# Four of eight batches: a hardware loop against the same passes written out

## The chip, the core and the metric

The kernel runs on one core of a Trainium2 chip. The metric is device time in microseconds (us); the kernel before takes 741.31 us, the median of three runs (741.03 to 741.88).

A core has five engines with an instruction stream each, synchronised by semaphores: TensorE (PE, with its weight loads shown as PEld), VectorE (DVE), ScalarE (ACT), GpSimd (POOL) and SyncE (SP), which here only issues transfers.

## The reference, cut to what matters

The input x is 8 batches of 1024 nodes with 128 features; adj is one 1024 x 1024 matrix that all batches share. Four layers follow one another in each batch, each added to its input and normalised over the 128 features:

```python
x = layernorm(x + L0(x, adj))   # (adj@x + x)@w0 + b0, rows scaled to length 1
x = layernorm(x + L1(x, adj))   # exp(8*tanh(q.k/sqrt(128)/8)) * adj, rows scaled to sum 1, @x @v
x = layernorm(x + L2(x, adj))   # (si + sj + adj*w_r + g_b) @ x @ w2 + b2
x = layernorm(x + L3(x, adj))   # relu(sum_k T_k(Laplacian of adj) @ x @ w3[k] + b3)
```

No batch depends on another, and every batch has the same work.

## The kernel before

The nodes are eight chunks of 128. Float32 products are made of float16 parts: `split_product` (lines 1113 to 1117) issues three matmuls for one product (high by high, high by low, low by high). TensorE therefore gets 7478 matmuls and as many weight loads.

Each engine has its own program, a function under `@block.sync`, `@block.gpsimd`, `@block.scalar`, `@block.vector` or `@block.tensor`. In each, a function `body(i, nxt, cur, prev, last)` issues one pass. Pass i is a software pipeline over three batches and a half: layer 0 of batch i+1 (flag `nxt`), the attention of batch i (`cur`), layers 2 and 3 of batch i-1 (`prev`), and the last residual and store of batch i-2 (`last`). The order of the instructions in a pass is written out by hand; engines meet only through semaphores, and nothing joins all of them between passes.

`iterations(eng, body)` (line 201) puts the passes in sequence: -1 fills the pipeline, 0, 1 and 2 are written out, 3 to 6 are one body in a hardware loop on each engine (line 208), and 7 is written out, followed by a written tail that drains the pipeline. Passes 2 and 3 to 6 have all four flags set, and their instructions are the same but for the values. Pass 1 still carries some Laplacian preparation.

Semaphores only count up over the whole run, so the value waited for grows with i:

```python
pe.wait_ge(S["pl"], t8 + t + 1)        # t8 = i * C, C = 8
```

On TensorE a pass begins with `scores(0)` (line 1207), the products of x1T and gr, shown as `r<-gr,x1T`. It ends with `apply_laplacian(r0, xq, ...)` (line 1382), shown as `r<-xq,lap`. So on TensorE the loop's branch lies between a matmul `r<-xq,lap` and a matmul `r<-gr,x1T`. On DVE a pass begins with `end_sum` (line 739) and `x0_max`, on ACT with the first tanh (line 391).

Of the kernel before, what the change touches and what calls it, by code (L numbers as in the profile page):

```python
# [12 lines left out]
B, N, D = 8, 1024, 128  # L29
# [62 lines left out]
def adj_resnorm(nc, x, adj, w0, b0, q, k, v, gw, gb, w2, b2, w3, b3, out):  # L92
    ctx = ExitStack()
    with ctx:
# [106 lines left out]
        def iterations(eng, body):  # L201

            body(-1, True, False, False, False)
            body(0, True, True, False, False)
            body(1, True, True, True, False)
            body(2, True, True, True, True)
            with eng.Fori(3, B - 1) as i:
                body(i, True, True, True, True)
            body(B - 1, False, True, True, True)  # L210

# [3 lines left out]
        @block.sync  # L215
        def _(sp):
            sp.dma_start(x0[:], x_v[0]).then_inc(S["x_in"], 16)
            adj_v = adj.rearrange("(c p) m -> c p m", p=P)
            for c in range(C):
                sp.dma_start(adj_rows[:, c, :], adj_v[c]).then_inc(adj_in[c], 16)  # L220
                if c == 1:
                    for dst, src in ((b0_bc[:], b0), (b2_bc[:], b2), (b3_bc[:], b3.rearrange("a b d -> (a b d)")),
                                     (wj_bc[:], gw[0:D]), (wi_bc[:], gw[D:2 * D]),
                                     (wr_gb[:, 0:1], gw[2 * D:2 * D + 1]), (wr_gb[:, 1:2], gb)):
                        sp.dma_start(dst, src.partition_broadcast(P)).then_inc(S["w_in"], 16)
            out_v = out.rearrange("b (c p) d -> b p c d", p=P)

            def body(i, nxt, cur, prev, last):
                if nxt and cur:
                    sp.wait_ge(S["e0"], i + 1)  # L230
                    sp.dma_start(x0[:], x_v[i + 1]).then_inc(S["x_in"], 16)
                if last:
                    sp.wait_ge(S["ln3_a"], i - 1)
                    sp.dma_start(out_v[i - 2], outb[:]).then_inc(S["stored"], 16)

            iterations(sp, body)
            sp.wait_ge(S["ln3_a"], B - 1)
            sp.dma_start(out_v[B - 2], outb[:]).then_inc(S["stored"], 16)
            for h, (first, end) in enumerate(END_PARTS):
                sp.wait_ge(S["ln3_v"], h + 1)  # L240
                sp.wait_ge(S["ln3_a"], B + h)
                sp.dma_start(out_v[B - 1][:, first:end], z_end.outb[:, first:end]).then_inc(S["stored"], 16)
            sp.wait_ge(S["stored"], 16 * (B + 1))
# [3 lines left out]
        def _(pool):  # L247
# [15 lines left out]
            def body(i, nxt, cur, prev, last):  # L263
# [14 lines left out]
                if cur:  # L278
                    norm_root(1, i)

            iterations(pool, body)
            norm_root(2, B - 2)
            norm_root(3, B - 3)
# [11 lines left out]
        def _(act):  # L295
# [68 lines left out]
            def body(i, nxt, cur, prev, last):  # L364
# [107 lines left out]
                if cur:  # L472
                    copy_x2(i)

            iterations(act, body)

            y2_hi(B - 2, 1)
# [992 lines left out]
```

## Time and profile before

| | |
|---|---|
| time, median of 3 runs | 741.31 us (741.03 to 741.88) |
| span of the profiled execution | 740.6 us |
| own time of the profiled execution | not given apart from its span; the median is 0.71 us above the span |
| PE busy | 648.8 us, 88% |
| DVE busy | 616.4 us, 83% |
| ACT busy | 384.0 us, 52% |
| POOL busy | 70.4 us, 10% |
| mean granted clock of TensorE | 0.959 of full |

The span runs from the first to the last instruction. A busy share is an average over all stages. Register, branch and semaphore instructions are not counted as busy; the view of one source line lists them under the engine's name with a q (PEldq is TensorE's sequencer). "issue" as the releaser of an idle time means that the profile shows no instruction of another engine that was waited for.

### The profile page before, as it was taken

How to read it: one execution, taken by the hardware profiler on the slowest of the kernel's cores; microseconds unless marked ns; L12 is line 12 of the kernel's file. 1: busy time of each engine (PE TensorE's matmuls, PEld its weight loads, DVE VectorE, ACT ScalarE, POOL GpSimd, SP SyncE). 2: the span in 40 equal slices, each digit the busy share in tenths (PEclk: the TensorE clock that was granted, in tenths of full speed). 3: DMA queues.
4: the chain of work that ended last, by engine and by line, in shares of the span. 5: the costliest groups of instructions: out<-in, count | busy, mean ns of one | idle time of the engine just before them, and what ended most of it. 6: DMA issues, size and time to landing. Idle time of an engine off the chain costs nothing.

```text
span 740.6 us, 17928 instructions
## 1 busy us (share of the span) xinstructions
PE 648.8 (88%) x7478; PEld 490.0 (66%) x7478; DVE 616.4 (83%) x1562; ACT 384.0 (52%) x525; POOL 70.4 (10%) x49
## 2 busy tenths in 40 slices
PE   3936955899999999999899998999899999949895
PEld 3533633566876687668757785668766786636894
DVE  3789898998989899989879896989788897887526
ACT  3828906763468255924395444915393447541302
POOL 0020001001200120011100210012000210020001
PEclk8989987999999999999999999999999999979998
DMA  8000000000100020002000020002000000001001
GB/s 264 38 29 1 1 1 29 1 1 2 31 2 1 1 59 2 2 1 59 4 1 2 1 59 2 2 1 58 4 1 2 22 10 1 2 1 30 2 3 58
DMA packets 20013, 14.59 MB, mean 20 GB/s; under 512 B 864, under 2 KB 18912, under 8 KB 19936
## 3 DMA queue, kind: packets, MB, share of 16 engines
q1 hardware_dynamic: 18816, 12.91, 5.9%
q8 instruction: 64, 1.05, 0.6%
q10 hardware_dynamic: 1120, 0.52, 0.2%
q14 instruction: 13, 0.11, 0.1%
HBM read 9.24 MB, written 4.19 MB: 18 GB/s over the span
## 4 chain that ended last, share of the span: by engine, by line
issue 42%; DVE 23%; PE 22%; ACT 5%; POOL 5%; DMA 1%; SPq 1%; POOLq 0%; ACTq 0%; DVEq 0%
POOL small L256 5%; PE r L1115 5%; PE r L1117 5%; PE r L1116 5%; DVE p_lo L791 3%; DVE att L786 3%; DVE stats L522 3%; ACT att L391 2%; DVE x L944 1%; DMA lap<-in_adj 1%; DVE x L561 1%; DVE lap L673 1%; PE m L1115 1%; PE m L1117 1%; PE m L1116 1%
## 5 line engine op out<-in xcount | busy, mean ns | idle before, releaser
L256 POOL TENSOR_TENSOR small<-small,minus_half 128x8 f32<-128x8 f32 x39 | 66.0, 1698 | 618.6 <-DVE small L544 494.8
L391 ACT ACTIVATE att<-r,coef 128x1024 f32<-128x1024 f32 x64 | 70.5, 1101 | 60.7 <-PE r L1117 60.4
L1229 PE MATMUL av<-vhi,p_hi 128*128 128x129 f16 x512 | 89.7, 220 | 6.9 <-DVE p_lo L791 6.5
L1232 PE MATMUL av<-vhs,p_lo 128*128 128x129 f16 x512 | 89.5, 220 | 0.0
L1231 PE MATMUL av<-vlo,p_hi 128*128 128x128 f16 x512 | 89.5, 219 | 0.0
L786 DVE TENSOR_TENSOR att<-att,adjT 128x1024 f32<-128x1024 f32 x64 | 78.1, 1220 | 10.8 <-ACT att L393 10.8
L791 DVE SCALAR_TENSOR_TENSOR p_lo<-p_hi,att 128x1024 f16<-128x1024 f16 x64 | 77.9, 1219 | 0.0
L1115 PE MATMUL r<-gr,lap 128*128 128x128 f16 x448 | 75.9, 219 | 0.0
L1117 PE MATMUL r<-gr,lap 128*128 128x128 f16 x448 | 75.8, 219 | 0.0
L1116 PE MATMUL r<-gr,lap 128*128 128x128 f16 x448 | 75.8, 219 | 0.0
L1115 PE MATMUL r<-xq,lap 128*128 128x128 f16 x448 | 75.4, 219 | 0.0
L1116 PE MATMUL r<-xq,lap 128*128 128x128 f16 x448 | 75.4, 219 | 0.0
L1117 PE MATMUL r<-xq,lap 128*128 128x128 f16 x448 | 75.4, 219 | 0.0
L303 ACT ACTIVATE p_hi<-att 128x1024 f16<-128x1024 f32 x64 | 66.8, 1044 | 6.5 <-DVE att L786 6.2
L393 ACT ACTIVATE att<-att 128x1024 f32<-128x1024 f32 x64 | 67.7, 1058 | 2.0
L1229 PEld LDWEIGHTS av<-vhi,p_hi 128*128 128x128 f16 x512 | 50.0, 98 | 19.9 <-DVE p_lo L791 15.7
L1115 PE MATMUL r<-gr,x1T 128*128 128x512 f16 x128 | 49.9, 390 | 11.5 <-issue 7.5
L331 ACT ACTIVATE x<-x,small 128x128 f32<-128x128 f32 x69 | 28.9, 481 | 50.6 <-DVE small L554 50.6
L1231 PEld LDWEIGHTS av<-vlo,p_hi 128*128 128x128 f16 x512 | 50.1, 98 | 4.2
L522 DVE BATCH_NORM_STATS2 stats<-x 128x6 f32<-128x128 f32 x248 | 51.7, 279 | 0.9
L1115 PE MATMUL m<-a_hi,x2s 128*128 128x512 f16 x128 | 49.3, 385 | 1.5 <-DVE r2b L700 0.8
L1232 PEld LDWEIGHTS av<-vhs,p_lo 128*128 128x128 f16 x512 | 50.1, 98 | 0.0
(294 smaller groups left out, 1932.0 us busy)
## 6 DMA issues: line engine op xcount, KB each, us to landing
x<-in_x SPq DMA_DIRECT2D x8, 512.0 KB, 4.4
lap<-in_adj SPq DMA_DIRECT2D x8, 512.0 KB, 9.6
out<-outb SPq DMA_DIRECT2D x7, 512.0 KB, 4.5
out<-att SPq DMA_DIRECT2D x1, 384.0 KB, 2.8
b_bc<-in_L_gnn_bias SPq DMA_DIRECT2D x3, 64.0 KB, 7.4
x<-in_L_gnn_weight ACTq DMA_DIRECT2D x1, 192.0 KB, 8.3
out<-att SPq DMA_DIRECT2D x1, 128.0 KB, 2.7
x<-in_L_gnn_q ACTq DMA_DIRECT2D x1, 64.0 KB, 4.1
```

Of the source, the lines that this page charges most:

```text
L256: return nc.gpsimd.tensor_tensor(dst, src, minus_half[:], ALU.pow)
L391: nc.scalar.activation(att[:, s], (r1, r0)[t % 2][:], ACT.Tanh, scale=c_tanh).then_inc(S["th"], 1)
L393: nc.scalar.activation(att[:, s], att[:, s], ACT.Exp, scale=TANH_CAP).then_inc(S["ex"], 1)
L522: l_ = nc.vector.bn_stats(stats[:, k_, j].rearrange("p a k -> p (a k)"), src[:, j])
L786: tt(att[:, s], att[:, s], adjT[:, t, :], ALU.mult).then_inc(S["pm"], 1)
L791: stt(p_lo[:, s], p_hi[:, s], -LO_UP, att[:, s], ALU.mult, ALU.add).then_inc(S["pl"], 1)
L1115: mm(dst, s_hi, m_hi, start=start, stop=False, skip_group_check=True)
L1116: mm(dst, s_hi, m_lo, start=False, stop=False, skip_group_check=True)
L1117: return mm(dst, s_lo, m_hi, start=False, stop=stop, skip_group_check=True)
L1229: mm(acc, p_hi[:, s, chunk(j)], vhi[:, t, 0:D + 1], start=(t == 0 and j % 3 == 0), stop=False, skip_group_check=True)
L1231: mm(acc[:, 0:D], p_hi[:, s, chunk(j)], vlo[:, t, :], start=False, stop=False, skip_group_check=True)
L1232: l_ = mm(acc, p_lo[:, s, chunk(j)], vhs[:, t, 0:D + 1], start=False, stop=(t == C - 1), skip_group_check=True)
```

## The change

The loop statement becomes a Python loop, so the four passes are issued one after the other with constant i, as the others are. Blank lines at the top of the file go too; they make no instruction.

```diff
             body(2, True, True, True, True)
-            with eng.Fori(3, B - 1) as i:
+            for i in range(3, B - 1):
                 body(i, True, True, True, True)
             body(B - 1, False, True, True, True)
```

It holds for all five engines, since all call `iterations`. The data instructions and their order stay; the loop's register moves, additions, compares and branches go, and every computed wait value becomes a constant.

## Rows read from the trace of the kernel before

**Rows 1.** The page's first part: busy us (share of the span) and instructions of each engine

```profile
PE 648.8 (88%) x7478; PEld 490.0 (66%) x7478; DVE 616.4 (83%) x1562; ACT 384.0 (52%) x525; POOL 70.4 (10%) x49
```

**Rows 2.** Waits of PE, 137 to 613 us: waiter <- releaser: total us, times, longest

```profile
PE r L1115 <- issue: 7.5, 3, 2.6
PE r L1121 <- DVE x L561: 5.8, 6, 1.0
PE r L1115 <- DVE yT L677: 3.3, 6, 0.5
PE av L1229 <- DVE p_lo L791: 1.7, 2, 1.2
```

**Rows 3.** Windows from each pass's first scores matmul to the next's, passes 2 to 6

```profile
core 0: us, PE busy (x) PEld busy (x) DVE busy (x) ACT busy (x) POOL busy (x), PEclk, DMA share, GB/s
209.20:287.80 78.60, 77.04 (x927) 58.63 (x925) 71.02 (x183) 43.83 (x61) 8.55 (x5) 1.00 0.06 15
287.80:369.15 81.35, 77.24 (x929) 58.57 (x925) 72.97 (x185) 43.83 (x61) 8.52 (x5) 1.00 0.05 15
369.15:451.69 82.54, 78.57 (x925) 59.14 (x925) 71.20 (x183) 44.06 (x61) 8.52 (x5) 0.98 0.06 14
451.69:534.41 82.72, 78.57 (x924) 59.01 (x925) 71.20 (x183) 43.83 (x61) 8.52 (x5) 0.98 0.05 14
534.41:613.10 78.69, 77.07 (x924) 58.61 (x925) 69.24 (x181) 43.82 (x61) 8.52 (x5) 1.00 0.03 8
```

**Rows 4.** Line 208, the loop: engine op: duration ns min/median/max, first and last start

```profile
L208 SPq COMPARE_BRANCH  x4: 40/45/50, 344.1 to 590.7; - x4
L208 POOLq COMPARE_BRANCH  x4: 40/45/54, 351.9 to 598.5; - x4
L208 ACTq COMPARE_BRANCH  x4: 40/45/54, 358.1 to 604.7; - x4
L208 DVEq COMPARE_BRANCH  x4: 50/60/67, 364.7 to 611.3; - x4
...
L208 PEldq COMPARE_BRANCH  x4: 76/3348/3473, 365.6 to 612.2; - x4
```

**Rows 5.** Line 208 again, 600 to 620 us: TensorE's branch that is not taken

```profile
L208 PEldq COMPARE_BRANCH  x1: 76/76/76, 612.2 to 612.2; - x1
```

**Rows 6.** Timeline of PE around the pass ends: start us, us, what [idle before <-releaser]

```profile
366.46 0.22 PE L1117 MATMUL r<-xq,lap 128*128 128x128 f16 x1
369.15 0.39 PE L1115 MATMUL r<-gr,x1T 128*128 128x512 f16 x1 [2.46 <-issue]
...
451.69 0.61 PE L1115 MATMUL r<-gr,x1T 128*128 128x512 f16 x1 [2.46 <-issue]
...
534.41 0.39 PE L1115 MATMUL r<-gr,x1T 128*128 128x512 f16 x1 [2.59 <-issue]
...
613.05 0.22 PE L1117 MATMUL r<-xq,lap 128*128 128x128 f16 x1
613.10 0.38 PE L1115 MATMUL r<-gr,x1T 128*128 128x512 f16 x1
```

**Rows 7.** Windows right behind the three taken branches, columns as in the passes' windows

```profile
369.40:372.80 3.40, 3.40 (x10) 1.20 (x9) 0.00 (x0) 1.02 (x1) 0.00 (x0) 0.50 0.02 5
...
451.30:454.70 3.40, 3.01 (x8) 1.10 (x9) 0.00 (x0) 0.16 (x1) 0.00 (x0) 0.50 0.02 5
...
534.40:537.80 3.40, 3.39 (x32) 1.95 (x33) 0.07 (x1) 1.77 (x2) 0.00 (x0) 1.00 0.02 5
```

**Rows 8.** DMA queue of instructions, 209.2 to 287.8 us (pass 2): packets, MB, share

```profile
q8 instruction: 7, 0.11, 0.6%
```

**Rows 9.** The same queue, 369.15 to 451.69 us (pass 4, ends in a taken branch)

```profile
q8 instruction: 9, 0.15, 0.7%
```

**Rows 10.** Windows of pass 1 and of the tail, columns as in the passes' windows

```profile
137.30:209.20 71.90, 68.71 (x869) 54.14 (x868) 66.89 (x159) 35.63 (x48) 6.92 (x4) 1.00 0.03 9
...
652.70:663.00 10.30, 4.99 (x38) 4.62 (x39) 9.13 (x41) 4.13 (x9) 3.95 (x3) 0.50 0.00 0
...
693.70:697.10 3.40, 3.40 (x36) 3.40 (x34) 1.88 (x4) 1.19 (x2) 0.00 (x0) 0.50 0.00 0
```

## The prediction

> **What bounds the kernel now.** I read the page's first part, then the waits of TensorE, then a table of windows with one row for each pass, and only then the loop's own instructions, line by line and in the timeline.
>
> The first part shows PE busy for 648.8 us and DVE for 616.4 us of a span of 740.6 [rows 1]. Both are near full, so the question in the middle of the program is which one gives the pace. The waits answer it: between 137 and 613 us PE stands still in only four kinds of places, and the largest sum, 7.5 us in three waits, has no releaser on another engine [rows 2]. The other three kinds are waits for DVE of at most 1.2 us. PE is the pace, with short hand-overs to DVE in it.
>
> The windows give the length of a pass, measured on PE from the first scores matmul of one pass to that of the next [rows 3]. Pass 2 is written out and takes 78.60 us. Pass 3, the first in the loop, takes 81.35, pass 4 82.54, pass 5 82.72, and pass 6, which leaves the loop without branching back, 78.69. They hold the same data instructions (924 to 929 recorded matmuls each, a few records may be missing). So three of the loop's passes are 2.7 to 4.1 us longer than a written one, and they are the three that end in a taken branch.
>
> Where does the time lie? Line 208 answers: on SP, POOL, ACT and DVE the loop's branch takes 40 to 67 ns all four times; on TensorE it takes 3348 ns in the median and 3473 at most [rows 4], and 76 ns the one time that it is not taken [rows 5]. PE's queue still has matmuls in it when the branch begins at 365.6, and runs them until the last start at 366.46; the first of the next pass starts at 369.15, and the timeline puts 2.46 us of idle time before it, with no releaser. The same at 451.69 (2.46) and 534.41 (2.59). At the loop's exit the last matmul starts at 613.05 and the next at 613.10: no gap [rows 6].
>
> **What the branch costs, in two terms and a small one.**
>
> First the stall. From start to start the gap is 369.15 - 366.46 = 2.69 us instead of 613.10 - 613.05 = 0.05, so 2.64 us are lost on the engine that gives the pace; the third, by its idle time, costs 0.13 more. Sum: 2.64 + 2.64 + 2.77 = 8.05 us.
>
> Second the clock. Behind the first two stalls the granted clock is 0.50 for 3.40 us, the lower of its levels (1.2 GHz, against 2.4), behind the third it stays at 1.00 [rows 7]. What that does is read from whole passes, since waits absorb part of it: pass 4 holds such a stretch and a stall, pass 3 a stall of the same 2.46 us alone: 82.54 - 81.35 = 1.19 us. Pass 5 has a stretch too and a stall longer by 0.13: 82.72 - 81.35 - 0.13 = 1.24. Sum: 2.43 us.
>
> Third the register instructions that compute wait values in each loop pass. Pass 6 has them and neither stall nor slow clock: 78.69 - 78.60 = 0.09 us, times four passes = 0.36. I take 0.09 as it stands, although the two windows were cut to a hundredth; between 0 and 0.2 per pass it would move the sum by -0.4 to +0.4.
>
> The terms add to 8.05 + 2.43 + 0.36 = 10.84. The same sum without splitting: passes 3 to 6 last 613.10 - 287.80 = 325.30, four written passes 4 x 78.60 = 314.40, difference 10.90 us [rows 3]. I use 10.90.
>
> **What lies beside the path.** The branch, addition and register set-up of SP, POOL, ACT and DVE go as well; at some 50 ns each, with DVE busy 71.02 of the 78.60 us of a written pass and the others less [rows 3], their ends are covered by PE's work, and I cost them at nothing beyond the 0.09. If that cover were gone, four engines by four times 0.05 is under 1 us in all. No transfer is moved against the data instructions; the stores and loads of batches come at the same place of each pass, only 3 to 4 us sooner.
>
> What is late next when the stall goes? That needs no model: pass 2 is exactly the pass that the four become, with its own waits inside it (some 1.0 us for the DVE normalisation and 0.5 for yT, once each per pass, [rows 2]). DVE has 7.6 us of slack per pass, so it doesn't become the bound.
>
> What is added is program text: three more passes of instructions on every engine. An executed instruction has to be fetched in either form. Pass 2, straight, brought 7 packets of instructions [rows 8], and pass 4, which jumps back, 9 [rows 9]. So written out there are fewer packets, not more, and no pass's code was kept from the last time. In pass 2 those 7 packets left no idle time without a releaser: all three such waits are at the branches [rows 2].
>
> The Trainium skill, page "Runtime: NRT & Kernel Launch", section "Instruction fetch mechanics", says that a taken branch out of the fetched window forces a fetch before the engine can go on, while sequential prefetch is mostly hidden. The rows above show both halves here (3348 ns taken, 76 ns not taken, no idle time in a straight pass), and the sum by this rule is the one above. The Trainium skill's page "Advanced Engine Details and Errata", section "Control Flow Timing", gives some 108 ns for a compare-and-branch; by it three back edges would cost 0.3 us and the kernel would take about 741.0. TensorE's 3348 ns disagrees with it; the 40 to 67 ns of the others don't.
>
> **The tail** is the same code. Its granted clock is 0.50 in 652.70 to 663.00 and again in 693.70 to 697.10 [rows 10], behind idle times of PE. The program reaches the tail 10.9 us sooner, and where such a stretch begins and ends need not shift by just that. One stretch of 3.40 us more or less costs or gives at most 1.2 to 1.7 us (1.2 as above; 1.7, half of 3.40, if PE is never waited out). I take zero and keep both ends.
>
> **Sum.** The span becomes 740.6 - 10.9 = 729.7 us. The profile names no time of its own beside the span; the median is 0.71 above it, and I leave that as it is: 741.31 - 10.90 = 730.4 us. The fast and slow ends of the three runs (741.03 to 741.88) differ by 0.85, about half of a stretch at half clock, so about +-0.5 belongs to any single median. The forecast's own range is 729.0 to 732.0.
>
> **The rivals.**
>
> A. Only the stall goes and the clock still falls. The reason would be that the granted clock drops about this often in a long dense stretch anyway. Against it: from 137.30 to 369.15, pass 1 to pass 3, it is at 1.00 without a break [rows 3, 10], and both falls stand right behind a stall. Time: 741.31 - 8.05 - 0.36 = 732.9; with one fall more, for the third pass end too, 734.1. Chance 0.09.
>
> B. The straight program is late in fetching, and slower. In the loop and out of it each packet is fetched anew, but the written passes place their instructions at new addresses. If a packet's arrival was late at some boundaries as it is behind the branch, each would cost the 2.64 us of a stall and perhaps 1.2 of clock. The gain of 10.9 is eaten by five late boundaries without a fall of the clock (5 x 2.64 = 13.2) or three with it (3 x 3.84 = 11.5). At one per pass with the clock's fall on each it is 4 x 3.84 = 15.4, and the time 745.8. For it: some 7 packets a pass mean 28 boundaries in the four passes. Against it: passes 1 and 2, straight and fetched the same way, show none [rows 2, 8]. Chance 0.03, with 0.01 more for a place of one or two late boundaries only, at 733 to 738.
>
> C. The time does not change: DVE or a hand-over takes up what PE gives back, as it would if the stall only covered another wait at the same place. Then passes 3 to 6 would stay at 81 to 83 us and the time within a few tenths of 741.3. Pass 6 in the loop without the stall ran in 78.69, which speaks against it; what it leaves open is that the written code doesn't come out as the same code (other waits merged or split). Chance 0.03.
>
> D. The tail's clock comes out otherwise, by one stretch or two: 728.0 to 729.0 or 732.0 to 733.8. For it: two stretches stand there, one of which (652.70 to 663.00) is far longer than the other. Against it: the idle times before them come from waits for DVE which don't change. Chance 0.12, even on both sides.
>
> **How the numbers follow.** The forecast has 0.72, A 0.09, B 0.04, C 0.03, D 0.12. The range for eight in ten holds the forecast, nearly all of D and the nearer half of A: 728.3 to 733.5. Changes of under 0.2%, some 1.5 us, can't be told from none here. A, D and the forecast are all faster by 1% or more; so faster 0.94, within 0.2% 0.03 (C), slower 0.03 (B).
>
> **What would show each step.** In the trace of the changed kernel: no instruction of line 208; no wait "PE <- issue" between 137 and 600 us, down from 7.5 us; passes 3 to 6 at 78.6 us each; the first scores matmul of pass 7 at 613.10 - 10.90 = 602.2; a granted clock of 1.00 from 137 to about 640 us; DVE, ACT and POOL with the same busy time within 1 us; some 5 to 7 instruction packets fewer. The forecast is wrong if a pass takes over 79 us: if with idle time of PE released by "issue", it is B, if at a granted clock of 0.50, A, if with more idle time released by DVE, C. If all passes are at 78.6 and the total is off, it is the tail, D.

## The result

The changed kernel takes 729.74 us, the median of four runs (728.46 to 730.62), against 741.6 us for the kernel before beside it: ratio 0.9833, 95% interval 0.9809 to 0.9857, 11.9 us less by the medians. A second comparison of the same two gave 731.07 and 743.02 us, ratio 0.9843 (0.9828 to 0.9859). The forecast was 730.4.

### The profile page after: what moved, and what is told of

It is laid out like the page before. It is cut to its first block, busy times and chain, and to the rows that moved or that the text cites. A ratio compares the mean times of both kernels' runs of the same rounds, so it can differ in the third digit from the quotient of the medians.

```text
span 726.3 us, 17483 instructions
## 1 busy us (share of the span) xinstructions
PE 644.0 (89%) x7478; PEld 487.4 (67%) x7478; DVE 615.4 (85%) x1562; ACT 383.9 (53%) x525; POOL 70.5 (10%) x49
## 4 chain that ended last, share of the span: by engine, by line
PE 48%; DVE 34%; ACT 9%; issue 4%; POOL 3%; DMA 1%; SPq 1%; ACTq 0%; DVEq 0%
PE r L1099 10%; PE r L1101 10%; PE r L1100 10%; DVE p_lo L775 5%; DVE att L770 4%; DVE stats L506 4%; ACT att L375 3%; POOL small L240 3%; DVE x L928 2%; PE m L1099 2%; PE m L1101 2%; PE m L1100 2%; DVE x L545 2%; PE av L1213 2%; PE av L1216 2%
## 5 line engine op out<-in xcount | busy, mean ns | idle before, releaser
L770 DVE TENSOR_TENSOR att<-att,adjT 128x1024 f32<-128x1024 f32 x64 | 77.9, 1218 | 10.9 <-ACT att L377 10.9
```

The costliest lines, as they stand in the source:

```text
L770: tt(att[:, s], att[:, s], adjT[:, t, :], ALU.mult).then_inc(S["pm"], 1)
```

## The profile after

The page of the changed kernel shows the same data instructions in less time:

```profile
span 726.3 us, 17483 instructions
PE 644.0 (89%) x7478; PEld 487.4 (67%) x7478; DVE 615.4 (85%) x1562; ACT 383.9 (53%) x525; POOL 70.5 (10%) x49
q8 instruction: 58, 0.95, 0.6%
q14 instruction: 19, 0.16, 0.1%
```

They answer to [rows 1]: the counts of data instructions are the same, PE is busy for 4.8 us less (it runs less at half clock), DVE for 1.0 us less, the span is 14.3 us shorter, and 445 fewer instructions are recorded: 489 register and branch instructions less, 44 semaphore instructions more.

The windows of passes 2 to 6, cut as in [rows 3], and the stretch from pass 7 to the end:

```profile
core 0: us, PE busy (x) PEld busy (x) DVE busy (x) ACT busy (x) POOL busy (x), PEclk, DMA share, GB/s
207.42:286.02 78.60, 77.05 (x928) 58.62 (x926) 70.99 (x183) 43.83 (x61) 8.55 (x5) 1.00 0.06 15
286.02:364.61 78.59, 77.05 (x927) 58.63 (x925) 70.98 (x183) 43.83 (x61) 8.54 (x5) 1.00 0.06 15
364.61:443.21 78.60, 77.05 (x927) 58.65 (x925) 70.97 (x183) 43.82 (x61) 8.55 (x5) 1.00 0.05 15
443.21:521.81 78.60, 77.06 (x928) 58.61 (x926) 70.95 (x183) 43.82 (x61) 8.55 (x5) 1.00 0.06 15
521.81:600.41 78.60, 77.05 (x928) 58.62 (x926) 70.96 (x183) 43.83 (x61) 8.55 (x5) 1.00 0.03 8
600.41:726.30 125.89, 103.42 (x1355) 84.17 (x1352) 83.73 (x222) 48.29 (x72) 10.19 (x7) 0.93 0.05 14
```

All five full passes take 78.59 to 78.60 us, at a granted clock of 1.00. Passes 3 to 6 last 600.41 - 286.02 = 314.39 us, against 325.30 before: 10.91 us. Where a branch stood, the timeline shows the next pass's first matmul 0.05 us behind the last one of the pass, against gaps of 2.46 to 2.59 in [rows 6]:

```profile
364.56 0.22 PE L1101 MATMUL r<-xq,lap 128*128 128x128 f16 x1
364.61 0.38 PE L1099 MATMUL r<-gr,x1T 128*128 128x512 f16 x1
```

The waits of PE between 135 and 600 us are those of [rows 2] without the first row, to 0.1 us:

```profile
PE r L1105 <- DVE x L545: 5.7, 6, 1.0
PE r L1099 <- DVE yT L661: 3.3, 6, 0.5
PE av L1213 <- DVE p_lo L775: 1.7, 2, 1.2
```

The clock stays at 1.00 for 502 us on end, and falls first in the tail:

```profile
135.50:637.20 501.70, 488.28 (x5821) 369.51 (x5819) 451.55 (x1123) 280.22 (x379) 49.66 (x29) 1.00 0.05 12
637.20:650.90 13.70, 5.60 (x43) 5.23 (x44) 11.68 (x60) 4.74 (x10) 4.90 (x3) 0.50 0.00 1
```

The other 3.4 us of the span's 14.3 lie outside these passes. Pass 2 begins at 207.42 and not 209.20 (1.78 us), and from pass 7 to the end it is 125.89 us, against 127.50 in the kernel before (1.61 us more):

```profile
613.10:740.60 127.50, 104.78 (x1355) 85.53 (x1352) 83.78 (x222) 48.20 (x72) 10.19 (x7) 0.92 0.05 14
```

Neither follows the change. In another profile of the changed kernel pass 2 began at 210.69, and the end took 127.5 us in a kernel whose TensorE passes are written out (e1) and 125.9 in one with all its loops (e3).

## The experiments

Every ratio is to runs of the kernel before taken beside it, on the same chip.

**TensorE's loop alone (e1_pe_written).** In `iterations`:

```diff
-            with eng.Fori(3, B - 1) as i:
-                body(i, True, True, True, True)
+            if eng.engine == nc.tensor.engine:
+                for i in range(3, B - 1):
+                    body(i, True, True, True, True)
+            else:
+                with eng.Fori(3, B - 1) as i:
+                    body(i, True, True, True, True)
```

> Only TensorE's four loop passes are written out; the other four engines keep their loops and register waits. Theory (the cost is TensorE's taken branch: stall plus clock): ratio 0.985 to 0.986, passes 3 to 6 at 78.6 to 78.7 us, no idle time of PE released by 'issue'; the branches of the other engines still 40 to 70 ns. Rival 1 (all engines' loops share the cost): about half of the gain, ratio near 0.993, passes over 80 us. Rival 2 (the straight code helps by its register-free waits on DVE): ratio near 1.0.

Measured: 731.02 against 743.14 us, ratio 0.9845 (0.9820 to 0.9870). The windows of passes 3 and 6:

```profile
288.00:366.70 78.70, 77.06 (x928) 58.59 (x925) 71.10 (x183) 43.82 (x61) 8.52 (x5) 1.00 0.06 15
...
524.05:602.73 78.68, 77.06 (x928) 58.60 (x925) 71.09 (x183) 43.81 (x61) 8.52 (x5) 1.00 0.03 8
```

The whole gain is there with four engines still looping. Rivals 1 and 2 fall.

**The other four engines alone (e2_others_written).** The same edit with `!=`.

> The other half: SP, POOL, ACT and DVE are written out, TensorE alone keeps its loop. Theory: ratio 0.999 to 1.001, three TensorE branches of 3.3 to 3.5 us, passes 3 to 5 at 81.3 to 82.8 us. Rival 1: ratio near 0.993. Rival 2: ratio near 0.986.

Measured: 742.16 us, ratio 0.9991 (0.9974 to 1.0008). TensorE's row of the loop's line, then the windows of passes 3 to 6:

```profile
L212 PEldq COMPARE_BRANCH  x4: 83/3635/3777, 367.5 to 614.8; - x4
```

```profile
289.81:371.27 81.46, 77.22 (x928) 58.65 (x925) 72.88 (x185) 43.83 (x61) 8.55 (x5) 1.00 0.05 15
371.27:454.16 82.89, 78.56 (x924) 59.12 (x925) 71.08 (x183) 44.17 (x61) 8.55 (x5) 0.98 0.05 15
454.16:537.10 82.94, 78.54 (x924) 59.09 (x925) 71.07 (x183) 43.87 (x61) 8.55 (x5) 0.98 0.06 15
537.10:615.71 78.61, 77.06 (x924) 58.63 (x925) 69.12 (x181) 43.83 (x61) 8.55 (x5) 1.00 0.03 9
```

All of the loss is kept by TensorE's loop alone. Pass 6 tells one thing more: it has TensorE's register instructions, and takes 78.61 us, while in e1, with those of the other engines, it took 78.68. So the forecast's 0.09 per pass lies with the other engines, and TensorE's computed wait values cost 0.01 at most. The taken branches are longer here than in the kernel before's profile and than expected (3.57, 3.70 and 3.78 us, in the trace, against 3.3 to 3.5), and the four passes last 325.90 us.

**The branch stays, its target is announced (e3_hint).**

```diff
-            with eng.Fori(3, B - 1) as i:
+            with nc.Fori(3, B - 1, engines=OrderedEngineSet([eng.engine]), hint_back_edge=True) as i:
```

```profile
L209 PEldq BRANCH_PREFETCH_HINT  x4: 31/31/45, 287.8 to 524.2; - x4
...
L209 PEldq COMPARE_BRANCH  x4: 80/226/252, 366.5 to 602.6; - x4
```

```profile
288.71:367.42 78.71, 77.06 (x928) 58.58 (x926) 71.08 (x183) 43.84 (x61) 8.52 (x5) 1.00 0.05 15
367.42:446.09 78.67, 77.05 (x927) 58.58 (x925) 71.09 (x183) 43.82 (x61) 8.52 (x5) 1.00 0.05 13
```

All loops, branches and register waits are still there; only the time that the branch waits for code is gone, 0.23 us in place of 3.35. This tells the fetch apart from the branch instruction itself. One thing was not expected. In passes 3 to 6 the queue q8 of instructions brought 6 packets here, 34 in the kernel before and 29 in the kernel after, in this order:

```profile
q8 instruction: 6, 0.10, 0.2%
```

```profile
q8 instruction: 34, 0.56, 0.7%
```

```profile
q8 instruction: 29, 0.48, 0.7%
```

**One taken branch in place of three (e4_one_branch).**

```diff
-            with eng.Fori(3, B - 1) as i:
+            for i in range(3, B - 3):
+                body(i, True, True, True, True)
+            with eng.Fori(B - 3, B - 1) as i:
                 body(i, True, True, True, True)
```

> Passes 3 and 4 are written out, 5 and 6 are a loop of two: one taken branch in place of three. Theory: one stall of 2.6 us and perhaps 1.2 of clock are left of 10.9: ratio 0.990 to 0.991 with a clock fall at the branch, 0.989 without; passes 3, 4 and 6 at 78.6 to 78.7 us, pass 5 at 81.3 to 82.7. Rival (a loop costs once, at its entry or exit, not per branch): ratio near 1.0.

Measured: 734.89 us, ratio 0.9897 (0.9870 to 0.9924). Passes 4, 5 and 6:

```profile
367.30:445.89 78.59, 77.05 (x927) 58.62 (x925) 70.98 (x183) 43.83 (x61) 8.55 (x5) 1.00 0.05 15
445.89:527.71 81.82, 77.23 (x927) 58.58 (x925) 72.92 (x185) 43.83 (x61) 8.58 (x5) 1.00 0.06 15
527.71:607.56 79.85, 78.33 (x924) 59.33 (x925) 69.31 (x181) 44.17 (x61) 8.52 (x5) 0.98 0.03 8
```

Pass 5 holds only the stall: 81.82 - 78.60 = 3.22 us, behind a branch of 3850 ns. Pass 6 holds only the stretch at half clock that followed (528.8 to 532.2 in the record of the granted clock): 79.85 - 78.69 = 1.16 us. The two terms stand apart here, and the second is the 1.19 and 1.24 of the forecast. The expectation had pass 6 at 78.6 to 78.7 us and missed that a fall behind the branch lands in it; the ratio is just under its 0.990.

**TensorE's branch moved (e5_cut_moved).** `body` on TensorE gets a parameter `part` that cuts a pass behind `adj_x2(1)`:

```diff
-            iterations(pe, body)
+            ...
+            body(2, True, True, True, True, part="early")
+            with pe.Fori(2, B - 2) as i:
+                body(i, True, True, True, True, part="late")
+                body(i + 1, True, True, True, True, part="early")
+            body(B - 2, True, True, True, True, part="late")
+            body(B - 1, False, True, True, True)
```

> All loops stay, without a hint; only the place of TensorE's branch moves: its loop now closes behind adj_x2(1), where the last matmuls issued are 24 and more of 512 columns (216 ns each) in place of 128-column ones (56 ns). In the kernel before, the branch began 1.05 us before the last queued matmul's end, some 19 matmuls. Theory (the 3.3 us are a fetch during which the queue runs on): the branches still take 3.3 us or more, but 19 matmuls of 216 ns are 4.1 us, so no idle time is left behind them, no fall of the clock, and the ratio is 0.985 to 0.988. Rival (a taken branch empties the queue or stops the engine wherever it stands): passes stay at 81 to 83 us, ratio 1.0.

Measured: 732.36 us, ratio 0.9865 (0.9841 to 0.9888). The branches, the place behind the first of them, and passes 3 to 6:

```profile
L1412 PEldq COMPARE_BRANCH  x4: 83/3394/3911, 294.5 to 532.1; - x4
```

```profile
297.16 0.38 PE L1117 MATMUL m<-a_hi,x2s 128*128 128x512 f16 x1
298.70 0.22 PE L1229 MATMUL av<-vhi,p_hi 128*128 128x129 f16 x1 [1.16 <-issue]
```

```profile
288.62:368.17 79.55, 76.88 (x928) 58.73 (x926) 71.30 (x183) 44.04 (x61) 8.52 (x5) 1.00 0.06 15
368.17:447.08 78.91, 76.87 (x927) 58.75 (x925) 71.21 (x183) 43.93 (x61) 8.51 (x5) 1.00 0.06 15
447.08:526.19 79.11, 76.88 (x927) 58.74 (x925) 71.20 (x183) 43.92 (x61) 8.52 (x5) 1.00 0.06 15
526.19:604.88 78.69, 77.06 (x927) 58.59 (x925) 71.13 (x183) 43.81 (x61) 8.51 (x5) 1.00 0.03 8
```

The branches take as long as ever, and of the forecast's 8.05 + 2.43 = 10.5 us only 0.86 + 0.22 + 0.42 = 1.5 us is left over a pass of 78.69. The queue's matmuls run on during the fetch, and 512-column ones last long enough to cover most of it. In one point the expectation missed: I counted 19 queued matmuls, 4.1 us of cover and no idle time. The trace shows 13 matmuls that start behind the branch's start at 294.52; the last of them ended at 297.54, 3.0 us behind it, and the branch took 3.91. No stretch at half clock followed these shorter stops.

**A short loop (e7_short_loop) and the filled gap (e6_fill_gap).** Both add 36 matmuls to the kernel after, in the tail's long idle time; their result is not read. The kernel e6 has them written out, e7 in a loop of nine turns of four.

```diff
             project(r0, yT, w2s[:, 0], w2s[:, 1]).then_inc(S["p2_mm"], 1)
+            for m in range(36):
+                mm(m7[:], a_hi[:, 0, 0:P], a_hi[:, m % C, 0:HALF], start=True, stop=True)
             x3_t(z_all, B - 2)
```

> The same 36 matmuls as a hardware loop on TensorE of nine turns of four: eight taken branches with a body of a dozen instructions. Theory (a taken branch is dear only if the code at its target is not there): each branch takes under 0.25 us, and the time is within 0.5 us of the variant without the loop. Rival (any taken branch costs 3.3 us): 8 x 3.3 = 26 us in a gap of 9, some 18 us slower.

Measured: 729.58 us in one run, with a span of 727.4 us; e6's is 727.5.

```profile
L1393 PEldq COMPARE_BRANCH  x9: 76/208/232, 635.1 to 639.8; - x9
```

Eight taken branches of 0.21 to 0.23 us: jumping back is cheap where the code of the target has just run.

> The kernel after with 36 matmuls of 512 columns added in the tail, where TensorE stands idle for 9.14 us behind the product of w2; their result is never read. Theory of the clock (it falls because TensorE stands idle): the granted clock stays at 1.00 through that gap, and the transposes and the products of w3 that ran 6.9 us at half clock get shorter; 1 to 2.5 us less than the kernel after, ratio to before 0.980 to 0.983. Rival (the tail waits for DVE, and TensorE's clock is off the path there): ratio as the kernel after's, 0.983 to 0.985.

Measured: 730.41 us, ratio 0.9844 (0.9825 to 0.9864). The timeline shows the fill and the transposes behind it:

```profile
635.88 7.93 PE L1394 MATMUL m<-a_hi 128*128 128x512 f16 x36
645.20 1.09 PE L1105 MATMUL r<-ident,x 128*128 128x128 f32 x8 [1.39 <-DVE x L545]
648.50 0.22 PE L1099 MATMUL av<-w3s,xq 128*128 128x128 f16 x1 [2.20 <-DVE xq L661]
```

The clock stayed at 1.00 through the gap and the transposes took 1.09 us, not the 1.97 of the kernel after. Nothing came of it: the products behind them wait for DVE either way (they start 46.87 us behind pass 7's start, against 46.86), and from pass 7 to the end it is 125.87 us, against 125.89. The rival's time held, but only half of its claim was tested, for the clock fell behind the transposes in e6 too:

```profile
648.50:653.00 4.50, 4.47 (x48) 4.29 (x48) 2.86 (x9) 3.15 (x6) 0.97 (x1) 0.62 0.00 0
```

So the half clock in the gap and in the transposes is off the path. The products of w3 ran at half clock in both kernels, and what that costs is not shown.

**Two passes per turn (e8_hint_two).** The others written out, TensorE in a hinted loop of two turns:

```diff
+                with nc.Fori(3, B - 1, 2, engines=OrderedEngineSet([eng.engine]), hint_back_edge=True) as i:
+                    body(i, True, True, True, True)
+                    body(i + 1, True, True, True, True)
```

> TensorE's loop holds two passes per turn (two turns, one taken branch) and carries the hint; the other engines are written out. With one pass per turn the hint brought the packets of instructions on the main queue from 64 down to 37, 27 fewer, nine for each jump back. If TensorE keeps the code of a pass and with the hint reads it where it lies, this is a matter of size: two passes are some 3,850 instructions, and if they don't fit there are 56 to 60 packets, as in the kernel after; if they are kept too, 40. The branch is under 0.3 us if the hint fetches the target ahead whatever the size, 3.3 us or more if it only works for code that is kept.

Measured, in the page's part on queues and in the rows of the loop's line:

```profile
q8 instruction: 60, 0.98, 0.6%
```

```profile
L213 PEldq COMPARE_BRANCH  x2: 88/236/385, 445.1 to 602.4; - x2
```

There are 60 packets, as if nothing were kept, and the taken branch is the one of 385 ns, more than the 0.3 us expected, but a tenth of a branch without the hint. Passes 3 to 6 take 78.61 to 78.62 us each. So the hint brings the target ahead for this size too, while the packets that e3 saved were not saved with a body twice as long; where the limit lies is not measured. Yet the one run took 734.63 us. The time is lost at the loop's exit: from pass 7 to the end it takes 129.65 us.

```profile
603.25 0.38 PE L1121 MATMUL r<-gr,x1T 128*128 128x512 f16 x1
606.18 0.39 PE L1122 MATMUL r<-gr,x1T 128*128 128x512 f16 x1 [2.55 <-issue]
```

```profile
603.25:732.90 129.65, 105.19 (x1355) 85.41 (x1352) 83.88 (x222) 48.65 (x72) 10.19 (x7) 0.91 0.05 14
```

One matmul past the loop TensorE stops for 2.55 us, and the clock falls to 0.50 for 3.4 us behind it (from 607.5). The last turn's hint had announced a jump that isn't taken; that the code behind the loop had to be fetched in its place is my reading, and no further run shows it. e3 has no such stop.

**Idle places at the start and end (e9_fill_head, e10_fill_tail, e11_after_again).** The kernel after with more unread matmuls: in e9 `fill(18)`, `fill(18)` and `fill(54)` ahead of three waits of passes -1 and 0, in e10 `fill(3)` and `fill(4)` around the tail's last transposes; e11 is the kernel after itself.

> The kernel after with unused matmuls of 512 columns in TensorE's three idle places at the start (18 and 18 in the pass that fills the pipeline, 54 in pass 0), where it waits 4.94, 4.74 and 13.14 us for DVE and the granted clock is 0.50 for 13.7 us twice. Theory (there TensorE's transposes and products stand between two works of DVE and so on the path): the clock stays at 1.00, the transposes in each place take 1.1 us in place of 2.0, and the first scores matmul of pass 2 comes 2 to 4 us earlier than in the kernel after of the same call; ratio to that kernel 0.994 to 0.998. Rival (off the path, as in the tail's first gap): no difference beyond 0.1%.

> The kernel after with seven unused matmuls around the last transposes in the tail (3 ahead, 4 behind), where TensorE waits 0.81 and 1.07 us for DVE. In the kernel before a stretch of 3.4 us at half clock followed these waits, in the kernel after's profile none; from the first scores matmul of pass 7 to the end it was 127.5 against 125.9 us. Theory (a fall behind those waits costs 1.6 us, whether it comes is chance, and with the gaps filled it doesn't): 125.9 us from pass 7 to the end, median 0 to 1 us under the kernel after's of the same call. Rival: no difference, or 0.3 us worse by the fills' own time.

> The kernel after, unchanged, as the comparison for the other two on the same chip: ratio to before 0.981 to 0.986, passes 2 to 6 at 78.6 us; from the first scores matmul of pass 7 to the end 125.9 us, or 127.5 if the clock falls behind the last transposes.

Measured: e9 729.78 us (729.24 to 731.56), e10 731.92 (731.12 to 732.68), e11 731.07 (730.27 to 731.94), the kernel before 743.02; ratios to it 0.9834 (0.9817 to 0.9852), 0.9852 (0.9834 to 0.9870) and 0.9843. Pass 0 in e9, then in e11:

```profile
61.79:122.82 61.03, 50.76 (x422) 30.36 (x423) 54.27 (x121) 37.48 (x45) 4.95 (x3) 1.00 0.03 10
```

```profile
61.83:125.35 63.52, 42.06 (x368) 27.04 (x369) 54.72 (x121) 37.56 (x45) 4.95 (x3) 0.87 0.03 9
```

At the start the clock appears to be on the path: pass 0 is 2.49 us shorter in these profiles and pass 2 begins 2.53 us sooner, as expected. But in the first profile of the kernel after pass 0 took 61.88 us, only 0.85 more than in e9, so the size is not settled. The median is 1.29 us under e11's, a ratio of 0.9982, just outside the expected 0.994 to 0.998, and the intervals to the kernel before overlap: e9 is not shown to beat the kernel after. e10 shows nothing: its median is 0.85 us over e11's, its tail takes 125.86 us, e11's 126.09 without the fills, and neither had a clock fall there. Whether the fills prevent one stays open.

## Why the prediction was right, step by step

**TensorE's taken branch is the place.** Shown by e1 and e2, one engine at a time, and by e4, where one branch is left and one pass pays.

**It is a stall of fetching code.** e3 keeps the branch and loses the wait; e7 branches without one; e5 keeps the wait and hides it behind long matmuls. The packets were forecast from q8 alone: there 58 instead of 64, the 5 to 7 fewer of the forecast. But the kernel before had fewer than the kernel after on the other queue of instructions:

```profile
q14 instruction: 13, 0.11, 0.1%
```

Together it is 77 packets in either form, so "fewer packets, not more" is wrong as a whole. e1 has 58 and 13, e2 64 and 19: q8 goes with TensorE's form, q14 with that of the other engines. So "no pass's code was kept from the last time" holds for TensorE alone. With their loops the other engines brought 3 packets in passes 3 to 6, written out 9. That their code was still there when they branched back fits their 40 to 67 ns, but no run makes one of them fetch.

**The sizes.** Stalls 8.05, clock 2.43, registers 0.36, by whole passes 10.90; the two profiles differ by 10.91 there. That the hundredths agree is no merit of the forecast: its 10.90 was read from the same profile that is compared here, and what it predicts is that all four passes become pass 2. The clock's term was 1.16 when measured alone. The register term went to the other engines (e1 against e2).

**Neighbours.** DVE did not become the bound; the written passes are pass 2 to 0.01 us. Rivals A, B and C fall together: no fall of the clock in 502 us, no late boundary in five passes, no new wait. One label of [rows 10] is wrong: pass 1 begins at 123.85 us, and its window there is the part from 137.30 on; the clock was at 0.50 for 3.4 us just ahead of it. Nothing in the sum hangs on that.

**What was not sized right.** The measured change of the medians is 11.9 us (11.95 in the second comparison), about 1 us more than the sum; the interval of the ratio holds 10.9 (10.9 / 741.6 is a ratio of 0.9853). That the forecast of the time missed by only 0.7 us is in part luck, since the kernel before came out 0.3 us slower beside it than in the forecast. Three things can make up the rest, and no run separates them. First, the stall was read from one profile, with branches of 3.34 to 3.47 us, while the seven others in e2, e4 and e5 took 3.29 to 3.91, 3.66 in the mean, 0.27 longer. Three times that is 0.8 us. Second, the third branch's stall had no clock fall in that profile, but may have one in other runs; of the seven stalls at pass ends in the kernel before, e2 and e4 five had one, though the third was spared in both profiles with three. Third, the fall in the tail, below, costs 1.6 us where it comes. So the forecast's terms may be a low sample.

The step from span to time was off too. I set 0.71 us between them, from a profile and the median of other runs; the profiled run of the kernel after took 728.46 us at a span of 726.3, that is 2.2, and e1's 1.8. It does not quite cancel in the difference either: time less span is 1.75 to 1.92 us in all 31 runs of the kernel before beside the experiments, and 2.12 to 2.21 in all nine of the kernel after. The changed form costs some 0.3 us outside the span, which the forecast put at nothing. By the medians of the spans, 741.1 and 728.9 us in the second comparison, the gain is 12.2 us, 1.3 more than the sum. The 0.3 us are in all ten runs of e2, where the other engines are written out, not in e1, and not in the one run of e8; what they are is not known.

**The tail (rival D) and the start.** The 1.6 us in the tail was the second fall, at 693.70 in [rows 10], which is on the path: 127.5 us from pass 7 on in the kernel before, e1, e2 and e5, which have it, and 125.8 to 126.1 in the kernel after, e3, e4, e6, e7, e9, e10 and e11, which don't. Why some runs have it isn't settled. Of the 1.78 us at the start 1.63 arise ahead of pass 0 (it begins at 61.83 before and at 60.20 after) and 0.14 in it. This part varies with the same kernel: pass 2 began at 207.42 in one profile of the kernel after and at 210.69 in the other. The forecast had pass 7 begin at 602.2; it began at 600.41, sooner by this start.

## What to carry to other kernels

Compare whole turns of a loop with a written-out turn: the difference is the price of going round, and the turn that leaves the loop tells what of it is the jump. A jump back over a long body costs the engine that sets the pace its fetch time less what is still queued, and on TensorE the clock behind it; the ways out are to write the turns out, to announce the branch, or to put the branch behind long instructions, and each gave nearly all of the gain here. On the other four engines the same loop cost 0.08 us per pass and no change of the time that could be told from none (e2), so code can stay short there. They have slack, and their branches took 40 to 67 ns.

## What the runs showed of the hardware that was not expected

- With the announced branch and one pass per turn, the 28 packets fewer on q8 (6 against 34) mean that TensorE's code of a pass was not brought again; with two passes per turn it was (60 packets in all). Without the announcement it was brought again even with one pass per turn.
- Leaving an announced loop can stall: 2.55 us one matmul behind it, in the one run of e8, and not in e3.
- In passes 2 to 6 stops of TensorE of 0.5 to 1.2 us were followed by no fall of the clock; of the eight stops of 2.46 to 2.97 us at pass ends (the kernel before, e2, e4, e8) six were. In the tail a fall came behind two stops of 0.8 and 1.1 us in four of twelve profiles, with the same stops in the others.
